# Pairing fields t and 20+t, a half tile for the lone field, and regrouped tiles in a CIN tower on one core

## The reference

```python
for idx, (W, b) in enumerate([(w0, b0), (w1, b1), (w2, b2)]):
    z = relu(einsum('bhd,bkd,hks->bsd', x0, xk, W) + b[None, :, None])
    if idx != 2:                 # half of the 128 maps feeds the next layer
        xk, out = z[:, :64, :], z[:, 64:, :]
    else:
        out = z
    direct.append(out)
logit = sum(concatenate(direct, axis=1), axis=-1)       # (2048, 256)
h = concatenate([logit, dense_ctx], axis=1)             # 272 wide
y = relu(relu(h @ W_top1 + b_top1) @ W_top2 + b_top2) @ W_top3
```

## Time and the profile before

| | |
|---|---|
| median of 3 runs | 2475.34 us (2474.52 to 2476.03) |
| the profiled execution | 2474.38 us |
| its span in the trace | 2472.6 us |
| instructions in the trace | 32417 |

### The profile page before, as it was taken

The page is one execution under the profiler, slowest core; times in us unless marked ns, Lnnn a source line. Parts: engine busy times, 40 slices in busy tenths (PEclk is TensorE's granted clock), DMA queues, the critical chain, the costliest instruction groups (busy, mean ns, idle before and its releaser), DMA issues. The chain is left out here.

```text
span 2472.6 us, 32417 instructions
## 1 busy us (share of the span) xinstructions
PE 2373.9 (96%) x8192; PEld 1539.6 (62%) x8192; DVE 2212.4 (89%) x2047; ACT 1364.1 (55%) x1532; POOL 2155.9 (87%) x1350
## 2 busy tenths in 40 slices
PE   1799999999999999999999999999999999999999
PEld 1466666666666666666666666666666666666665
DVE  2689999999999999999999999999999999999983
ACT  2355555555555555555555555555555555555552
POOL 4799999999999999999999999999999999999640
PEclk9899999999999999999999999999999999999999
DMA  7888888888878888888888788888888878888710
GB/s 179 187 187 207 196 185 211 212 173 209 207 186 194 210 209 176 204 211 181 203 204 209 177 204 212 181 206 205 201 180 208 214 177 208 208 188 191 199 55 1
DMA packets 398547, 467.04 MB, mean 189 GB/s; under 512 B 170337, under 2 KB 179553, under 8 KB 398257
## 3 DMA queue, kind: packets, MB, share of 16 engines
q1 hardware_dynamic: 299202, 302.30, 54.3%
q10 hardware_dynamic: 78848, 159.39, 24.7%
q0 software_dynamic: 20480, 5.15, 1.8%
HBM read 457.03 MB, written 9.71 MB: 189 GB/s over the span
## 5 line engine op out<-in xcount | busy, mean ns | idle before, releaser
L458 POOL TENSOR_TENSOR low<-prod_pool,high 128x1024 fp32r<-128x1024 f32 (+1 forms) x640 | 1532.5, 2395 | 88.8 <-ACT high L775 73.2
L775 ACT ACTIVATE high<-prod_pool 128x1024 fp32r<-128x1024 f32 (+1 forms) x640 | 677.3, 1058 | 733.5 <-DVE prod_pool L516 695.9
L627 PE MATMUL z<-prod_whole,w_whole 128*128 128x512 f32 (+1 forms) x2176 | 1011.5, 594 | 5.6 <-DVE prod_whole L516 5.6
L627 PE MATMUL z<-high,w_high 128*128 128x512 f32 (+1 forms) x1920 | 939.5, 489 | 55.9 <-ACT high L775 55.9
L627 PE MATMUL z<-high,w_low 128*128 128x512 f32 (+1 forms) x1920 | 758.6, 395 | 0.0
L429 POOL DMA_INDIRECT rows<-table,index x640 | 611.5, 955 | 147.8 <-issue 99.0
L516 DVE TENSOR_TENSOR prod_whole<-xh,x 128x1024 f32<-128x1024 f32 x512 | 620.5, 1212 | 110.1 <-PE z L627 90.8
L627 PE MATMUL z<-low,w_high 128*128 128x512 f32 (+1 forms) x1920 | 614.0, 401 | 33.5 <-POOL low L458 33.3
L627 PEld LDWEIGHTS z<-prod_whole,w_whole 128*128 128x128 f32 (+1 forms) x2176 | 412.7, 190 | 355.7 <-issue 296.8
L516 DVE TENSOR_TENSOR prod_pool<-xh,x 128x1024 f32<-128x1024 f32 x512 | 621.3, 1213 | 10.0 <-POOL low L458 10.0
L627 PEld LDWEIGHTS z<-high,w_high 128*128 128x128 f32 (+1 forms) x1920 | 363.6, 189 | 229.2 <-issue 141.1
(11 more groups left out here) (45 smaller groups left out, 365.5 us busy)
## 6 DMA issues: line engine op xcount, KB each, us to landing
xh<-x_rows SPq DMA_DIRECT2D x64, 2560.0 KB, 16.5
xh<-x_rows ACTq DMA_DIRECT2D x64, 2432.0 KB, 20.6
xb<-x_rows SPq DMA_DIRECT2D x128, 546.0 KB
xb<-x_rows SPq DMA_DIRECT2D x64, 468.0 KB
xa<-x_rows SPq DMA_DIRECT2D x192, 78.0 KB
rows<-table,index POOLq DMA_INDIRECT x640
x_rows<-rows SPq DMA_DIRECT2D x256, 20.0 KB
xh<-staged SPq DMA_DIRECT2D x2, 1280.0 KB, 6.9
```

The lines of the kernel that those rows point to most:

```text
L458: pool.tensor_tensor(low[0:g.rows, g.split_slot, 0:n, :], prod_pool[0:g.rows, g.slot, 0:n, :], high[0:g.rows, g.split_slot, 0:n, :].bitcas ...
L627: return pe.matmul(z[stage][:, :], weights[0:g.rows, table[stage, t], :], src[0:g.rows, i, :], start=t == 0 and weights is not w_low and s ...
L775: act.activation(high[0:g.rows, g.split_slot, 0:n, :], src[0:g.rows, 0:n, :], ACT.Copy).then_inc(high_ready, 1)
```

## The change

- Fields t and 20+t share a tile (before: 2t and 2t+1). `x0_rows` is laid out chunk by chunk, so the 20 (or 19) fields of one half of `xh` are one contiguous run for a partition, loaded in pieces of at most 8 KB (`load_run`).
- Tile 19 holds field 19 in both halves, in place of a field and a pad. It is a half tile: the rounded product stays on partitions 0 to 63 of `high`, and VectorE writes the low part over partitions 64 to 127 of the same buffer. Two matmuls do the contraction, with w_high in both halves and with w_low, whose upper half is zero. The memsets of the pads are gone.
- The groups and kinds of all tiles are listed anew. Layers 1 and 2 have 11 groups (before 10), seven of them split. GpSimd has 9 groups a chunk (before 10).
- Slots: whole 4, GpSimd's products 3, high and low 4 (before 3, 2, 5).
- On GpSimd the index addition stands at the start of the chunk, ahead of the first low part, and is no longer right ahead of the gather that uses it.
- A class `Chunk` replaces the pair (c, p); at the end the MLP's context inputs move from the product buffers to the weight buffers.

SUM_AFTER, LAST_OUT_AFTER, XA_AFTER and FIRST_OUT_AFTER keep their values 9, 5, 4, 5.

```diff
-KINDS = {
-    0: [BY_POOL, BY_DVE, BY_POOL, WHOLE],
-    1: [WHOLE, BY_POOL, WHOLE, BY_DVE, BY_POOL, WHOLE, BY_POOL, BY_DVE, BY_POOL, WHOLE],
+GROUPS = {
+    0: [(BY_POOL, 0, 2), (BY_DVE, 2, 2), (WHOLE, 4, 2), (WHOLE, 6, 1)],
+    1: [(WHOLE, 0, 2), (BY_DVE, HALF_TILE, 1), (BY_POOL, 2, 2), (WHOLE, 4, 2), (BY_DVE, 6, 2),
+        (BY_POOL, 8, 2), (WHOLE, 10, 2), (BY_POOL, 12, 2), (BY_DVE, 14, 2), (BY_POOL, 16, 2),
+        (WHOLE, 18, 1)],
 }
-WHOLE_SLOTS, POOL_SLOTS, SPLIT_SLOTS = 3, 2, 5
+WHOLE_SLOTS, POOL_SLOTS, SPLIT_SLOTS = 4, 3, 4
...
-    x0_dram = nc.dram_tensor("x0_rows", (XROWS, N), f32, kind="Internal").ap()
+    x0_dram = nc.dram_tensor("x0_rows", (CHUNKS * XROWS, CN), f32, kind="Internal").ap()
...
+        def load_run(engine, c, part, tiles, field):
+            of = rows_of(c)
+            n = len(tiles)
+            spread = bass.AP(tensor=of.tensor, offset=of.offset + field * CN,
+                             ap=[[0, H], [1, n * CN]])
+            into = xh[c.p][part * H:(part + 1) * H, tiles[0]:tiles[0] + n, :]
+            engine.dma_start(into.rearrange("p t n -> p (t n)"), spread,
+                             max_dma_last_dim=RUN_BYTES).then_inc(xh_loaded[c.p], 16)
...
-                load_fields(sp, c, p, 0)
+                load_run(sp, c, 0, range(0, TK), 0)
+                load_run(sp, c, 1, range(HALF_TILE, TK), HALF_TILE)
...
-            def begin_gather(c, p):
-                pool.wait_ge(ids_loaded[p], 8 * (c - p) + 16)
-                pool.tensor_tensor(index[p][:, :], ids_sb[p][:, :], row_base_sb[:, :],
+            def make_index(c):
+                pool.wait_ge(ids_loaded[c.p], 8 * (c.n - c.p) + 16)
+                if not c.known or c.n >= 2:
+                    pool.wait_ge(stored[c.p], 8 * STORES * (c.n - c.p))
+                pool.tensor_tensor(index[c.p][:, :], ids_sb[c.p][:, :], row_base_sb[:, :],
                                    ALU.add).then_inc(index_ready, 1)
...
+                if ahead:
+                    make_index(ahead[0])
                 for i, (g, at) in enumerate(mine):
                     low_parts(g, at)
...
+                part = slice(H, 128) if g.half else slice(0, g.rows)
+                into = (high if g.half else low)[part, g.split_slot, 0:n, :]
                 dve.tensor_tensor(
-                    low[0:g.rows, g.split_slot, 0:n, :], prod_dve_v[0:g.rows, 0:n, :],
-                    high[0:g.rows, g.split_slot, 0:n, :].bitcast(f32), ALU.subtract,
+                    into, prod_dve_v[part, 0:n, :],
+                    high[part, g.split_slot, 0:n, :].bitcast(f32), ALU.subtract,
                 ).then_inc(low_by_dve, 1)
...
+                    elif g.half:
+                        wait_count(pe, made, c, g, g.of_kind + 1, g.kind)
+                        both = high[:, g.split_slot, :, :]
+                        mm(w_high, SPLIT_TILE, both, 0, True)
+                        done = mm(w_low, SPLIT_TILE, both, 0, last=True)
...
-                load_fields(act, c, p, 1)
+                load_run(act, c, 1, range(0, HALF_TILE), TK)
```

More of the change, by code:

```diff
@@ L75, in __init__ @@
     def __init__(self, stage, chunk, g, counts):
[L76 to L80, removed]
+        of = GROUPS[stage]
+        self.stage, self.chunk, self.g = stage, chunk, g
+        self.kind, first, n = of[g]
+        self.tiles = range(first, first + n)
+        self.begins_layer, self.ends_layer = g == 0, g == len(of) - 1
+        self.half = stage > 0 and first == HALF_TILE
+        self.rows = 128 if stage else (LAST0 if first == T0 - 1 else JT * F)
         self.split = self.kind != WHOLE
@@ L98, in plan @@
         order += [(1, c)] + [(0, c + 1)] * (c + 1 < CHUNKS) + [(2, c)]
[L99 removed]
+    return {(stage, c): [Group(stage, c, g, counts) for g in range(len(GROUPS[stage]))]
             for stage, c in order}
@@ L107, with __init__, __add__, __sub__ @@
 LIKE = 2
[L109 to L114, removed]
+ALL_KINDS = [kind for groups in GROUPS.values() for kind, _, _ in groups]
+PER = {"all": len(ALL_KINDS), "split": sum(k != WHOLE for k in ALL_KINDS),
+       BY_POOL: ALL_KINDS.count(BY_POOL), BY_DVE: ALL_KINDS.count(BY_DVE)}
+assert 2 * (PER["all"] - PER["split"]) % WHOLE_SLOTS == 0
+assert 2 * PER[BY_POOL] % POOL_SLOTS == 0 and 2 * PER["split"] % SPLIT_SLOTS == 0
+class Chunk:
+    def __init__(self, n, like):
+        self.n, self.like = n, like
+        self.known = isinstance(n, int)
+        self.p = like % 2
+    def __add__(self, k):
+        if self.known:
+            return Chunk(self.n + k, self.n + k)
+        return Chunk(self.n + k, LIKE + (self.like + k) % 2)
+    def __sub__(self, k):
+        return self + -k
 WHOLE_TILE, SPLIT_TILE = {}, {}
@@ L432, in gather, with chunk @@
                 ).then_inc(gathered[p], 16)
-            def chunk(c, p):
-                known = isinstance(c, int)
-                gathers = [(c + 3, 1 - p)] if not known or c + 3 < CHUNKS else []
-                if known and c == 0:
-                    gathers.insert(0, (2, 0))
-                left = [(at, q, j) for at, q in gathers for j in range(GATHERS)]
+            def chunk(c):
+                ahead = [c + 3] if not c.known or c.n + 3 < CHUNKS else []
+                if c.known and c.n == 0:
+                    ahead.insert(0, c + 2)
+                left = [(at, j) for at in ahead for j in range(GATHERS)]
                 stages = [(1, c), (0, c + 1), (2, c)]
-                if known and c == CHUNKS - 1:
+                if c.known and c.n == CHUNKS - 1:
                     stages.pop(1)
                 mine = [(g, at) for s, at in stages for g in groups(s, at) if g.kind == BY_POOL]
+                if ahead:
+                    make_index(ahead[0])
                 for i, (g, at) in enumerate(mine):
@@ L448, in chunk @@
                     for _ in range(-(-len(left) // (len(mine) - i))):
-                        at, q, j = left.pop(0)
+                        at, j = left.pop(0)
                         if j == 0:
-                            begin_gather(at, q)
-                        gather(q, j)
+                            if at is not ahead[0]:
+                                make_index(at)
+                            begin_gather(at)
+                        gather(at.p, j)
             def low_parts(g, c):
@@ L760, in copy_xa @@
             def copy_xa(c):
-                act.wait_ge(x0_loaded, (c + 1) * 2 * JT * 16)
-                if not (isinstance(c, int) and c == 0):
+                act.wait_ge(x0_loaded, (c.n + 1) * 2 * JT * 16)
+                if not (c.known and c.n == 0):
                     wait_made(act, 0, c - 1)
@@ L829, in _ @@
             act.wait_ge(cols_loaded, 16)
-            load_odd_fields(0, 0)
-            copy_xa(0)
-            round_stage(0, 0)
-            layer_out(0, 0)
+            load_odd_fields(Chunk(0, 0))
+            copy_xa(Chunk(0, 0))
+            round_stage(0, Chunk(0, 0))
+            layer_out(0, Chunk(0, 0))
             over_chunks(act, chunk)
@@ L860, in _ @@
             round_inputs(0)
-            layer_out(2, CHUNKS - 1)
+            layer_out(2, Chunk(CHUNKS - 1, CHUNKS - 1))
             for m in range(MSTEPS):
```

248 lines of the change are left out of this document (120 added, 128 removed).

## The result

| | before | after |
|---|---|---|
| median | 2474.93 us (4 runs, 2473.32 to 2476.03) | 2564.02 us (4 runs, 2563.19 to 2566.00) |
| the profiled execution, its span | 2474.38, 2472.6 | 2566.00, 2564.2 |

A forecast was written before the change was run, and what follows sets the result against it. GpSimd, never idle at 36.2 us a chunk, was the bound. 88.5 (start) + 40.9 (chunk 0) + 59 x 37.27 + 3 x 36.5 + 93.0 (end) + 1.8 = 2532.6, so 2533 us; own range 2505 to 2558, 8-in-10 range 2472 to 2562.

The forecast's parts named there:

- The order on ScalarE: Seven split groups put copy_xa and layer_out ahead of roundings, making GpSimd's input late; period 37.27 us, 1.07 more.
- S: Time at which VectorE begins a chunk's layer 2 products, 1.65 us after TensorE ends layer 1.
- P16: Tiles 16 and 17; in layer 2 their rounding queues behind layer_out(0), GpSimd's low part beginning at S + 16.2.
- GpSimd's chain to layer 1: GpSimd's work from P16's low part of layer 2 to that of layer 1, 15.62 us with a second gather.
- VectorE's own loop: VectorE's steps over one period: 14.97 + 15.52 + 5.2 = 35.7 us, so it waits about 1.5 at S.
- The start: Chunk 1's loads and xa come sooner with fewer pieces: 4 us taken, S of chunk 0 at 88.5.
- D14: Tiles 14 and 15; copy_xa ahead of their rounding makes VectorE's low part in layer 1 about 0.55 us late.
- Rival 1: GpSimd's chain does not end last: period 36.5, 2487 us, 0.5% slower; chance 0.15.
- Rival 2: P16's lateness is not on the loop; VectorE bounds at 35.7: 2436 us, 1.6% faster; chance 0.15.
- Rival 3: Field loads land late, over 36 us, and set each period; at 38 us 2580; chance 0.04.
- Rival 4: The slots or ScalarE's order add a stall that was missed: above 2560 us; chance 0.04.
- Transfers: Field loads landing in 16.5 us stay hidden by 18 or more; long runs might make them some 8 shorter.

The follow-up runs named there:

- b_index: The kernel before with only the index addition, and its wait for the stores of the rows, moved to the start of the chunk: 2450.40 us, ratio 0.9902.
- b_hooks: The kernel before with only ScalarE's actions hung one split group earlier (constants 9, 4, 3, 4), the changed kernel's late order: 2579.56 us, ratio 1.0427.
- a_gather: The changed kernel with the second gather in a slot moved from layer 1 to layer 2, where GpSimd is idle: 2523.82 us, ratio 1.0199.
- a_lowtop: The changed kernel with the half tile's low part made on partitions 0 to 63 into an unread buffer, so left out of the result: 2548.2 us.
- after_again: The changed kernel run once more, unedited, to check its start: 2561.75 us.
- a_2kb: The changed kernel, same layout, with its long runs read in pieces of 2 KB: 2561.21 us.
- a_all: The changed kernel with constants 10, 6, 5, 6 (ScalarE's actions and VectorE's sum later) and the second gather moved to layer 2: 2497.51 us, ratio 1.0094.
- a_both: The changed kernel with constants 9, 6, 5, 5 plus FIRST_OUT_AFTER 6 (the sum not moved) and the second gather moved to layer 2: 2525.42 us.

## Why the prediction was wrong in size and right in kind

- **What bounds the kernel before**: right. b_index takes 0.54 us of GpSimd's wait away and the period falls by 0.39.
- **The order on ScalarE**: right, and shown alone by b_hooks. In after the sum comes at S + 14.02 (13.77), `direct` at 14.73 (14.48), P16's rounding at 15.44 (15.08), GpSimd's low part at 16.58 (16.2).
- **GpSimd's chain to layer 1**: 15.52 (15.62); from there to the next S 5.55 (5.45). Its end in last place is shown by a_gather and by the last three periods, without gathers: 36.96, 36.92 and 36.83, where 36.5 was forecast.
- **Two terms of the period were mis-sized.** "The nearest row is the 512-column sum, 0.59, and I take 0.6 for all three" holds for the two short products but not for the short low part, which with the step ahead of it takes 0.24 more; a_lowtop shows this and its cause. And P16's rounding starts 0.71 after `direct`, not 0.6: 0.11. As both layers have a short low part, VectorE's own loop was mis-sized too: 37.66 - 1.42 (its mean idle at S) = 36.24, where 35.7 was forecast, from terms for layer 1 and layer 0 that no row gave. The misses of 0.10 in GpSimd's chain and in the way to S cancel. 16.58 + 15.52 + 5.55 = 37.65, and 0.24 + 0.11 is nearly all of the 0.39 between 37.66 and 37.27.
- **The start: "the most that fewer pieces can give is 7.6, the least 0: I take 4".** The bound of 0 was the right end. S(0) was 97.34 against 88.5; after_again and a_2kb put 4.7 of the 8.8 on this step and the rest on the one execution. The period of chunk 0, 40.64, was forecast as 40.9, and the end, 2564.2 - 2470.82 = 93.4, as 93.0.
- **The sum**: 8.8 (start) - 0.3 (chunk 0) + 59 x 0.39 + 1.2 (the last three) + 0.4 (end) = 33 us, which is 2564.2 less 2530.8. The range missed by 2 us since it gave the period 0.35 to both sides and the start nothing beyond 4. The same kernel taken again (after_again, 2561.75) lies just inside it, so the 2 us say little; the 31 us against the forecast do.
- **TensorE's waits**: in layer 0 and layer 1 as forecast (1.26 for 1.3, 0.70 for 0.8). The wait in layer 2, forecast as nearly gone, is there with 0.67: P16's low part comes 0.4 later than forecast. VectorE waits 1.4 at S (1.5), and its low part of D14 is 0.44 late (0.55).
- **Rival 1** (period 36.5): fell; GpSimd's chain ended last, by 0.69 (37.66 less a_gather's 36.97) where I had 0.76. **Rival 2** (faster, VectorE at 35.7): fell, and more deeply than I had it, since even a_all, with order, sum and gather put right, has a period of 36.52. **Rival 3** (late loads): fell; no wait for x_rows is on the path of a period. **Rival 4** names a time above 2560, and the time is there, but not for its reason: the one stall forecast as nearly none, TensorE's 0.67 in layer 2, follows from the terms that were too small.
- **Transfers**: hidden, as forecast; that longer pieces might be shorter loads was wrong. The rule that I weighed (the Trainium skill, DMA: Bandwidth & Descriptors, Specifications) would have an engine of the 16 move 27 GiB/s; the windows show 14.2 GB/s with pieces of 8 KB and 20.9 with 2 KB, and they decide. By that figure, which is 29.0 GB/s, the load would have been 7.1 us shorter, an estimate, and not 8: 16.5 x (1 - 16.5 / 29.0).

What stays open: why the long pieces take more engine time, why the stores began 4 to 5 us later at the start, and which of VectorE and GpSimd's chain to TensorE holds a_all at 36.52.

## What to carry to other kernels

Where actions are hung on the index of a group, adding a group moves them all: list each constant with what it must stand behind and ahead of, for a relieved engine gains nothing while the queue that feeds it holds its input back. Before moving work, count the chains that lie within half a microsecond of the period: here moving one ReLU or moving one gather won the same 40 us, both together (a_both) no more, and only with the fourth constant as well was it 67 (a_all). And try the small part alone: moving one addition of 0.22 us away from its user won 1% on the kernel before, while the whole change, which has this move too, lost 3.6%.

## What the runs showed of the hardware

- A subtraction of VectorE (64x512) that starts at partition 64 between products that start at partition 0 costs 0.12 us on each side, since neither overlaps with it; the same instruction on partitions 0 to 63, or on all 128, costs nothing beyond its own step of 0.60.
- Reading the same 159 MB took 27.4% of the DMA engines' time in 33792 packets and 20.1% in 78848, with the rows laid out chunk by chunk; with the old layout it took 24.7% in 78848. After and a_2kb took the same time.
- The ACTIVATE of `direct` in layer 0 (64x512, 0.69 us busy) is followed by P16's rounding 0.71 us later, so without an overlap. Other steps of ScalarE do overlap: in after, that of `last` (128x512, 0.67 busy) is followed 0.57 later. `direct` lies on partitions 64 to 127 there and the rounding starts at 0, as with VectorE's short low part; no run tests whether that is the cause here.

```profile
1258.62 0.67 ACT L768 ACTIVATE last<-z,cols_sb 128x512 f32<-128x512 f32 x1
1259.19 1.06 ACT L801 ACTIVATE high<-prod_pool 128x1024 fp32r<-128x1024 f32 x1
```
